# One-expert network: PE's two layers two and four steps behind the transpose, four banks and buffers in place of two

## The reference, cut to what matters

```python
def _L1_ffn_ref(x, wr, br, w1, b1, w2, b2):
    scores = jnp.einsum('bsh,he->bse', x, wr) + br
    expert_id = jnp.argmax(scores, axis=-1)
    h = jnp.einsum('bsh,ehf->ebsf', x, w1) + b1[:, None, None, :]
    h = jax.nn.gelu(h, approximate=False)
    y = jnp.einsum('ebsf,efh->ebsh', h, w2) + b2[:, None, None, :]
    one_hot = jax.nn.one_hot(expert_id, E, dtype=x.dtype)
    return jnp.einsum('ebsh,bse->bsh', y, one_hot)
...
x = x + _L1_ffn_ref(_layernorm(x, axis=-1), ...)
```

## Time and profile before

| | us |
|---|---|
| median of three runs (lowest, highest) | 1872.3 (1870.96, 1874.24) |
| the profiled execution's own time | 1877.03 |
| its span, first to last instruction | 1875.2 |
| the stage `one_expert_ffn` in it | 1634 to 1869, 235.0 |
| mean granted clock, span and stage | 0.932 and 0.85 |

### The profile page before, as it was taken

The page is one execution under the profiler, slowest core; times in us unless marked ns, Lnnn a source line. Parts: engine busy times, 40 slices in busy tenths (PEclk is TensorE's granted clock), DMA queues, the critical chain, the costliest instruction groups (busy, mean ns, idle before and its releaser), DMA issues. The chain is left out here.

```text
span 1875.2 us, 63422 instructions
## 1 busy us (share of the span) xinstructions
PE 1620.9 (86%) x24719; PEld 1365.9 (73%) x24719; DVE 1422.6 (76%) x3215; ACT 952.6 (51%) x2012; POOL 1408.6 (75%) x1270
## 2 busy tenths in 40 slices
PE   4999999999989364999999999999997688277776
PEld 3888888777778253778888888888886588277676
DVE  6988888888876914889898888888885756755554
ACT  3777887777763323454454544444443610344443
POOL 3887787988975554899999998888885267766654
PEclk9999999999999576999999999999999789588888
DMA  8000050000000414444444343433342364522211
GB/s 256 12 10 9 9 190 14 20 17 17 18 8 1 135 38 123 114 115 116 122 108 108 96 97 97 97 97 97 97 98 49 92 216 145 171 65 62 61 57 35
DMA packets 155077, 154.08 MB, mean 82 GB/s; under 512 B 37246, under 2 KB 106944, under 8 KB 154160
## 3 DMA queue, kind: packets, MB, share of 16 engines
q1 hardware_dynamic: 128912, 125.14, 24.7%
q0 software_dynamic: 6704, 15.61, 2.9%
q10 hardware_dynamic: 19312, 11.48, 2.3%
HBM read 58.77 MB, written 26.71 MB: 46 GB/s over the span
## 5 line engine op out<-in xcount | busy, mean ns | idle before, releaser
L1455 POOL TENSOR_TENSOR wa_rot<-wa_rot,wa_cross 128x1024 f32<-128x1024 f32 x128 | 306.9, 2397 | 44.1 <-DVE wa_cross L1673 43.0
L417 POOL TENSOR_TENSOR sa_sd<-sa_sd,sa_mx 128x1024 f32<-128x1024 f32 x128 | 245.2, 1916 | 78.2 <-DVE sa_mx L665 77.8
L1670 DVE TENSOR_TENSOR wa_rot<-wa_ps_qk,cos 128x1024 f32<-128x1024 f32 x128 | 155.6, 1216 | 36.8 <-PE wa_ps_qk L1521 36.7
L1620 ACT COPY wa_pt<-wa_ps_svt 128x1024 f32<-128x1024 f32 x64 | 64.9, 1015 | 220.7 <-PE wa_ps_svt L1557 220.7
L665 DVE TENSOR_REDUCE sa_mx<-sa_sd 128x16 f32<-128x1024 f32 x128 | 154.8, 1209 | 0.0
L1461 POOL TENSOR_TENSOR wa_sd<-wa_sd,wa_mx 128x1024 f32<-128x1024 f32 x64 | 121.8, 1904 | 34.2 <-DVE wa_mx L1686 33.8
L545 PEld LDWEIGHTS sa_ps_o<-sa_vbd,sa_pt 128*64 128x64 f32 x4096 | 135.0, 138 | 11.5 <-issue 8.1
L1521 PE MATMUL wa_ps_qk<-wa_xt,l_wk 128*128 128x128 f32 x1024 | 134.5, 286 | 9.7 <-DVE wa_cross L1673 9.5
L545 PE MATMUL sa_ps_o<-sa_vbd,sa_pt 128*64 128x18 f32 x4096 | 139.2, 210 | 1.8 <-DVE sa_o L694 1.8
L1521 PE MATMUL wa_ps_qk<-wa_xt,l_wq 128*128 128x128 f32 x1024 | 134.2, 285 | 6.4 <-DVE wa_cross L1673 4.1
L534 PE MATMUL sa_ps_st<-ident,sa_sd 128*128 128x128 f32 x1024 | 135.8, 276 | 3.7 <-ACT sa_sd L606 1.5
(11 more groups left out here) (313 smaller groups left out, 4307.0 us busy)
## 6 DMA issues: line engine op xcount, KB each, us to landing
wa_whole<-wa_rot SPq DMA_DIRECT2D x1024, 64.0 KB, 2.0
choice_dram<-sa_zero_rows SPq DMA_DIRECT2D x32, 256.0 KB, 3.2
choice<-choice_dram ACTq DMA_DIRECT2D x22, 256.0 KB, 4.0
x_res<-in_x_dram SPq DMA_DIRECT2D x16, 256.0 KB, 6.7
sa_ctx_t<-in_ctx_t_dram SPq DMA_DIRECT2D x64, 64.0 KB, 1.8
c_index<-in_index_dram SPq DMA_DIRECT2D x2, 2048.0 KB, 7.7
xn_dram<-c_xn SPq DMA_DIRECT2D x16, 256.0 KB, 3.0
cs_ctx_t<-in_ctx_t_dram SPq DMA_DIRECT2D x16, 256.0 KB, 2.9
```

What stands on the lines that cost most here:

```text
L417: pool.tensor_tensor(sd[:, v % 4], sd[:, v % 4], mx[:, v % 4].unsqueeze(2).to_broadcast([P, H0, SEQ]), ALU.subtract).then_inc(sub_ready, 1)
L1455: pool.tensor_tensor(rot[n][:, v % 2], rot[n][:, v % 2], cross[n][:], ALU.add)\
L1670: dve.tensor_tensor(rot[n][:, v % 2].rearrange("p f j t -> p (f j) t"), src.rearrange("p f j t -> p (f j) t"), bc(k.cos[:], 1, 2 * QUADS), ...
```

## The change

xt, hid and ps_h get four buffers instead of two, which makes eight PSUM banks instead of six. On PE, hidden comes two steps behind the transpose (one before) and output four (two before); on ACT the gelu comes two steps behind the copy (one before); on DVE add_up comes four steps behind copy_weights (three before). The waits for free buffers and the lags of the loops follow. wt, xb, ps_x, ps_y, xg and y keep their sizes, and POOL its order.

```diff
-        xt = sb("xt", [P, 2, P])
-        hid = sb("hid", [P, 2, FF, P])
+        xt = sb("xt", [P, 4, P])
+        hid = sb("hid", [P, 4, FF, P])
...
-        ps_h = [c.enter_context(nc.psum_tensor(f"m1_h{n}", [P, FF, P], F32)) for n in range(2)]
+        ps_h = [c.enter_context(nc.psum_tensor(f"m1_h{n}", [P, FF, P], F32)) for n in range(4)]
...
             def hidden(t, v):
                 pe.wait_ge(xt_ready, t + 1)
                 pe.wait_ge(wt_ready, t + 1)
-                if late(t, 2):
-                    pe.wait_ge(hid_ready, t - 1)
+                if late(t, 4):
+                    pe.wait_ge(hid_ready, t - 3)
...
             def step(i, u):
-                for stage, behind in ((transpose, 0), (hidden, 1), (output, 2)):
+                for stage, behind in ((transpose, 0), (hidden, 2), (output, 4)):
...
-            pipeline(pe, NS, step, 2, DEEP)
+            pipeline(pe, NS, step, 4, DEEP)
...
             def x_copy(t, v):
                 act.wait_ge(xt_made, t + 1)
-                if late(t, 2):
-                    act.wait_ge(h_made, t - 1)
+                if late(t, 4):
+                    act.wait_ge(h_made, t - 3)
...
             def gelu(t, v):
                 act.wait_ge(h_made, t + 1)
-                if late(t, 2):
-                    act.wait_ge(y_made, t - 1)
+                if late(t, 4):
+                    act.wait_ge(y_made, t - 3)
...
-                for stage, behind in ((x_copy, 0), (gelu, 1)):
+                for stage, behind in ((x_copy, 0), (gelu, 2)):
...
-            pipeline(act, NS, step, 1, DEEP)
+            pipeline(act, NS, step, 2, DEEP)
...
-            for i in range(NS + 3):
+            for i in range(NS + 4):
                 if i < NS:
                     copy_weights(i, expert)
                 if i + 1 < NS:
                     expert = expert_of(i + 1)
-                if i >= 3:
-                    add_up(i - 3)
+                if i >= 4:
+                    add_up(i - 4)
                 if i < NS:
                     add_bias(i)
```

More of the change, by code:

```diff
@@ L2291, in hidden @@
                 pe.wait_ge(wt_ready, t + 1)
-                if late(t, 2):
-                    pe.wait_ge(hid_ready, t - 1)
+                if late(t, 4):
+                    pe.wait_ge(hid_ready, t - 3)
                 for f in range(FF):
-                    mm = pe.matmul(ps_h[v % 2][:, f], w1[:, v % 4, f * P:(f + 1) * P], xt[:, v % 2], start=True, stop=True)
+                    mm = pe.matmul(ps_h[v % 4][:, f], w1[:, v % 4, f * P:(f + 1) * P], xt[:, v % 4], start=True, stop=True)
                 mm.then_inc(h_made, 1)
@@ L2302, in output @@
                 for f in range(FF):
-                    mm = pe.matmul(ps_y[v % 2][:, 0:P], hid[:, v % 2, f], w2[:, v % 4, f], start=(f == 0), stop=(f == FF - 1))
+                    mm = pe.matmul(ps_y[v % 2][:, 0:P], hid[:, v % 4, f], w2[:, v % 4, f], start=(f == 0), stop=(f == FF - 1))
                 mm.then_inc(y_made, 1)
             def step(i, u):
-                for stage, behind in ((transpose, 0), (hidden, 1), (output, 2)):
+                for stage, behind in ((transpose, 0), (hidden, 2), (output, 4)):
                     if has(i - behind, NS):
                         stage(i - behind, (u - behind) % DEEP)
-            pipeline(pe, NS, step, 2, DEEP)
+            pipeline(pe, NS, step, 4, DEEP)
         @block.scalar
@@ L2316, in x_copy @@
                 act.wait_ge(xt_made, t + 1)
-                if late(t, 2):
-                    act.wait_ge(h_made, t - 1)
-                act.copy(xt[:, v % 2], ps_x[v % 2][:, 0:P]).then_inc(xt_ready, 1)
+                if late(t, 4):
+                    act.wait_ge(h_made, t - 3)
+                act.copy(xt[:, v % 4], ps_x[v % 2][:, 0:P]).then_inc(xt_ready, 1)
             def gelu(t, v):
                 act.wait_ge(h_made, t + 1)
-                if late(t, 2):
-                    act.wait_ge(y_made, t - 1)
+                if late(t, 4):
+                    act.wait_ge(y_made, t - 3)
                 for f in range(FF):
-                    op = act.activation(hid[:, v % 2, f], ps_h[v % 2][:, f], ACT.Gelu, bias=b1[:, v % 4, f:f + 1])
+                    op = act.activation(hid[:, v % 4, f], ps_h[v % 4][:, f], ACT.Gelu, bias=b1[:, v % 4, f:f + 1])
                 op.then_inc(hid_ready, 1)
             def step(i, u):
-                for stage, behind in ((x_copy, 0), (gelu, 1)):
+                for stage, behind in ((x_copy, 0), (gelu, 2)):
                     if has(i - behind, NS):
                         stage(i - behind, (u - behind) % DEEP)
-            pipeline(act, NS, step, 1, DEEP)
+            pipeline(act, NS, step, 2, DEEP)
         @block.vector
```

## The result

The changed kernel took 1886.1 us (median of 7 runs, 1879.4 to 1892.4) against 1872.3 of the kernel before; the ratio is 1.0068, interval 1.0052 to 1.0083: slower by 0.7%, some 13 us. In the profiled executions (1892.41 against 1877.03) nearly the whole difference lies in this stage, 14.3 of 15.4 us: from the first gather to the end of the last scatter it takes 248.9 us (1635.53 to 1884.43), where it took 234.6 (1634.46 to 1869.05).

A forecast was written before the change was run, and what follows sets the result against it. The prediction took late signals from PE, and how much lateness each order absorbs, as the bound. Weights and banks 0, fill +1.3 and tail -0.3 gave +1 us: 1873 us, range 1846 to 1894.

The forecast's parts named there:

- What bounds the kernel: Stage of 235 us: no engine full; PE's results reach ACT and DVE 1.26 to 5.83 us late.
- the gelu's cover: PE's work between hidden and output of a tile: free lateness grows from 0.7 to 2.6 us.
- The weights: Hidden waits for DVE's weight copy, which waits for output: free time falls from 2.4 to 0.55 us; net 0, chance 0.36.
- the tighter of the two decides: Of the free times for gelu and weights, 0.7 and 2.4 us before, 2.6 and 0.55 after, the smaller sets the time.
- The signs set for a slow result: On PE: hidden's idle time above 60 us and a lower clock.
- the step on fill, tail and POOL: Stage's start and end, and POOL's scatter: +1.3 us fill, -0.3 tail, 0 for the later add; together +1 us.
- the step on them: More h banks and hid buffers: no wait for a bank ends idle time before PE or ACT, so 0.
- Fill and tail: First output follows two more hidden layers, +1.3 us counted; last output no longer waits for its gelu, -0.3.
- the slower one: Output's lateness hits PE's hidden through the weights: 27.3 us less 7, +20, giving 1892; chance 0.23.
- the faster one: Deeper order absorbs the lateness; POOL becomes the bound at 1822, or 1848 with stalls halved; chance 0.27.
- PE itself late: PE's matmuls themselves end as late as their signals, so reordering saves nothing; 1873 us, chance 0.14.

The follow-up runs named there:

- DVE's order alone: The kernel before with one edit: DVE adds up four steps behind the weight copy in place of three; 1892.0 us, ratio 1.0109.
- one tighter wait: The kernel before with POOL's gather of tile t waiting for the transpose of tile t-4 in place of t-8; 1859.0 us, ratio 0.9937.

## Why the prediction was right or wrong, step by step

*What bounds the kernel:* right in that lateness of PE's signals decides, and the gelu's cover grew as worked out: output's waits for it, 12.7 us, went to 0.3. The rows also held what was not read from them: POOL's DMAs run into the stall with 0.30 us between them.

*The weights:* the wait came where it was forecast. The copy has idle time that ends with output, hidden starts 0.10 us after the copy, output no longer waits. But the step's conclusion, that "the tighter of the two decides", failed: with the add three behind, the room is smaller still, 0.55 less an add and a bias add of 0.28 each, and the time is that of the kernel before. PE's wait for the copy is paid while PE would wait for late signals anyway. The signs set for a slow result, hidden idle above 60 us and a lower clock, came (65.8, 0.83), but hidden's idle time is not the cause: 53.3 us of it cost nothing there.

*Where the forecast broke:* the step on fill, tail and POOL, which took the add for "one PE step later", with "some four steps of slack: 0". This term is +13.6 us by the medians (1886.1 against 1872.6 with the add three behind; as ratios to the kernel before, 1.0068 and 0.9995). The prediction named add_up as standing behind the waiting copy and POOL's scatter as waiting for it, and then counted PE steps where the wait is for a late signal: at each stall the copy puts 1.27 us (1690.79 to 1692.06) between that signal and the add. With some 17 stalls of 14 us that is some 22 us. The slack was not there in the kernel before either: POOL was idle 72.5 us in front of its scatter, 38.2 of them put down to DVE, a row that the step left out.

*The path from the add to the loss.* Output waits 0.3 us in the changed kernel, so it is not y_ready for the ps_y banks (by name such waits are 0.7 us with DVE's order alone, but 12.1 with hidden two and output three steps behind, where they may take part); the weights come no later than with the add three behind, since the copy starts on the signal itself. What is left is the scatter, and with it the gather behind it on POOL: its waits are 16 to 25 us longer in each kernel that has this order. The traces show this path too. A pause of the changed kernel with the add three behind, DVE:

```profile
1715.90 0.29 DVE L2360 TENSOR_TENSOR m_y<-m_y,m_xb 128x128 f32<-128x128 f32 x1 [3.83 <-remote]
```

POOL in the same pause:

```profile
1713.77 0.98 POOL L2263 DMA_INDIRECT m_xg<-xx_dram,gather_idx  x1 [0.30 <-issue]
1717.02 1.01 POOL L2269 DMA_INDIRECT out_dram<-m_y,scatter_idx  x1 [2.27 <-DVE m_xb L2353]
```

The last gather ends at 1714.75, the late signal starts the add 1.15 us later, and the scatter comes 1.12 us after the add's start. In the changed kernel's stall above, the last gather ends at 1689.28, the signal starts the copy 1.51 us later, the add follows 1.27 us behind, and the scatter again 1.11 us after the add. So POOL stands 3.89 us where it stood 2.27, and 1.27 of the 1.62 more are the copy. The changed kernel with eight weight buffers does the same eight DMAs, four tiles, between two pauses, but no copy waits in front of its add; POOL:

```profile
1734.45 1.01 POOL L2269 DMA_INDIRECT out_dram<-m_y,scatter_idx  x1 [2.38 <-DVE m_xb L2353]
...
1747.13 1.01 POOL L2269 DMA_INDIRECT out_dram<-m_y,scatter_idx  x1 [2.52 <-DVE m_xb L2353]
```

Its round takes 12.7 us in place of 14.0 to 14.1; some 17.75 rounds in 71 tiles make that 24 us, and the stages differ by 23.9 (248.9 - 225.0). With the add three behind, POOL pauses more often, mostly every three tiles (9.8 us from the scatter at 1707.25 to that at 1717.02), so the changed kernel loses less against it. No run delayed the scatter alone, and why the run of DMAs has three tiles in one kernel and four in another stays open.

*The rule on the banks.* The runs with eight banks, four weight buffers and the old place of the add are at 0.9998 and 0.9995, so the banks and the deeper order together give 0, as the step on them said. The rule of the Trainium skill that all eight PSUM banks be in use (Perfetto Trace Analysis, "Matmul Optimizations") finds no support in these two runs, and the trace of after names no wait that a bank ends. With eight weight buffers the new order and its banks do come with a gain (0.9965), which eight weight buffers alone do not bring (0.9993); no run tells the banks from the order there.

*Fill and tail:* the first add comes 14.3 us after the first gather, 12.8 before (1635.53 to 1649.87, 1634.46 to 1647.30), +1.5 where +1.3 was counted. The agreement is luck: 1.27 of it is the copy that now stands in front of the first add (1648.60 to 1649.87), which was not counted; the two hidden layers that were counted added next to nothing to the wait.

*The rivals:* the slower one had the time nearly right and its price from the wrong place: DVE's waits for output stayed at 107 us, and the idle time before PE's two layers rose by 11.1 us (55.0 to 66.1), not by 27.3, while 53.3 us before hidden alone cost nothing with the add three behind. In the faster one, stalls were to halve by a deeper order; with eight weight buffers the deeper order does gain, but 6 us, not 25. "PE itself late" is not told apart from late signals by any run here.

The forecast named a change of the stage by more than 8 us as what would overturn it. It was 14.3.

## What to carry to other kernels

When a loop is given another depth, list for each result that moves not only who computes it but everybody who waits for it, on the queues that seem to have room too, and put on an in-order engine nothing short and awaited behind something long that waits for the same signal. And where an engine that runs ahead is followed by late signals of another, try holding it back: one tighter wait (13.8 us less) gave more here than the new order with two more banks and eight weight buffers (some 6 us less).

## What the runs showed of the hardware

With two indirect DMAs for each tile, PE's results reach the other engines up to 5.83 us after their modelled end in the stall of rows 5 and 6, and 6.56 us in that of the changed kernel. With one a tile none of ACT's waits put down to PE before a gelu is longer than 1.4 us (2.1 where POOL fills a buffer), and between 1700 and 1712 PE is busy without a break. Leaving out either kind brings the stage from 235 to some 146 us and its granted clock from 0.85 to 0.96 or 0.97. POOL filling a buffer for as long as a gather does not make the signals late, two gathers do. The late signals come free about when POOL's run of DMAs ends: in the pauses of POOL above 1.5 us between 1645 and 1845 (kernel before, changed kernel, and this with the add three behind or with eight weight buffers) the signal reaches DVE 0.7 to 1.9 us after the end of POOL's last DMA, with one exception in 66. Through what part of the chip the one holds up the other stays open, and also whether PE's work itself is late or only the news of it.
